# A graph transformer on one NeuronCore: the edges' places come as one row and are spread over the partitions by PE

## The chip, the cores and the metric

One core of a Trainium2 chip. The metric is the device time of one execution, in microseconds, the median of three runs. The profile is of one more execution. Engines: PE (TensorE), DVE (VectorE), ACT (ScalarE), POOL (GpSimd), SP (SyncE, which here only issues DMAs).

## The reference

Two layers of a heterogeneous graph transformer over 6250 nodes (128 features, 8 heads of 16) and 100,000 edges sorted by target, then a projection, a residual and a layer norm. What matters here is the part over edges:

```python
kw = kT[src, :, etype]
m = vT[src, :, etype]
a = jnp.einsum('ehd,ehd->eh', kw, q[dst]) * pri[:, etype].T / SQRT_D
att = edge_softmax(a, dst, n)          # exp(a - max over the edges of dst) / sum of these
msg = (m * att[:, :, None]).reshape(-1, H * HS)
hag = jax.ops.segment_sum(msg, dst, num_segments=n)
```

## The kernel before

Each layer has a matrix stage (`fused`: the tables of keys and values by node and relation, and q, by tiles of 128 nodes) and an edge stage (`attend`). The change touches the edge stage alone.

Edges stand in slots of 128, each slot with edges to the nodes of one tile of 128. Four slots are a quad, eight quads a block, and each layer has 26 blocks, so 208 quads (`NQUADS`), 416 in both layers. The five engines run their own instruction streams through the quads in order and meet on semaphores. For a quad q of a block:

- POOL (L793) gathers four times 128 rows of 1 KB from the table into `rows`, which holds three blocks (`DEPTH`), 24 quads. Before it refills a quad's place it waits for `sum_psum` of 24 quads before (L791).
- SP (`load_places`, L609) loads for each quad the place of each edge in its node tile, 512 bf16 numbers, the same for all 128 partitions, by one DMA of 128 KB with a broadcast source, into a ring of four (`DST_RING`). Per block it also loads two arrays of flags (L602).
- DVE compares these numbers with the partition's number (`turned`, L1750) and so makes `onehotT`, 128 x 512 f32, in a ring of two. It does it for quad q+2 in its step for q.
- PE multiplies that with the tile's q rows (`fetch_q`, L1268), which gives the q of each edge in bank 1 or 2, and tells `q_psum`. In its step for q it does the fetch of q+1.
- DVE multiplies the gathered keys with them (`multiply`, L1742), sums by head (L1755), and some quads later weighs the values (`weigh`, L1764).
- ACT makes the one-hot matrices by edge (L1012, L1015), PE sums the weighed rows into node rows (`sum_quad`, L1281, two pairs of slots a quad, each telling `sum_psum`) 13 quads after their product, DVE adds them to `sums` (L1779).
- In quads 0 to 5 of each block, the maxima over the edges of each node for the block before: DVE's scans, and five small groups of matmuls on PE, some into bank 3 and some into bank 4 (L1295, L1311, L1319, L1325, L1332).

DVE's step for a quad has four places in this order: the product; at place 0 an add, then `turned` for q+2; at place 1 an add and the head sums; at place 2 an add; at place 3 an add and the weighing. A piece of the maxima comes at some of these places.

## Time and profile before

| | us |
|---|---|
| median of three runs (lowest, highest) | 4215.57 (4210.69, 4224.35) |
| the profiled execution | 4224.53, its span 4222.7 |
| busy in the span: PE | 2457.1 (58%) |
| DVE | 2713.9 (64%) |
| ACT | 1710.2 (40%) |
| POOL | 2537.3 (60%) |

Busy shares are means over matrix stages and edge stages, which have different limits, so each is to be read by stretch. "x1664" is a count; behind the first bar of a grouped row stand the busy time in us and the mean ns of one, behind the second the idle time of the engine just before these instructions and what ended it. "remote" stands where the semaphore that ended the wait was updated at a time at which no instruction of the trace ends; "issue" where nothing is seen that was waited for. A `x8` in a timeline row merges eight instructions: an f32 matmul counts twice, so four matmuls are eight.

### The profile page before, as it was taken

Reading aid. Unit: us, or ns where it says so; the run is one execution under the profiler, and the core shown is the slowest. Engines: PE = TensorE matmul, PEld = TensorE weight load, DVE = VectorE, ACT = ScalarE, POOL = GpSimd, SP = SyncE. Lnnn points to the kernel's source line nnn. Section 1 sums busy time; section 2 is a strip of 40 time slices with the busy share of each in tenths; the row PEclk is TensorE's granted clock in tenths of the full one; section 3 lists DMA queues with packets and bytes.
Section 4 is the critical chain, followed back from the end, with each engine's and each line's share of the span. In section 5 each row is a group of like instructions: output and inputs, shape, how many; then the busy total and the mean of one; then the engine's idle time right before and its main releaser. Section 6 shows DMA issues by size and latency. Waiting matters only on the chain.

```text
span 4222.7 us, 54460 instructions
## 1 busy us (share of the span) xinstructions
PE 2457.1 (58%) x12785; PEld 1801.8 (43%) x12786; DVE 2713.9 (64%) x6706; ACT 1710.2 (40%) x3970; POOL 2537.3 (60%) x2596
## 2 busy tenths in 40 slices
PE   3777771455565555656677776145655555555365
PEld 2333331345454545545333333144554545444343
DVE  6676671466676666667678887156666666666465
ACT  2676670233323333324566666023323333323255
POOL 4666657466666666661566664746666666666426
PEclk8899895677777777777789899567777777777666
DMA  8999984344444444434799998434434344444131
GB/s 197 409 414 410 417 338 146 89 119 119 117 128 117 119 117 116 118 113 107 241 383 380 406 398 327 129 88 115 119 111 113 112 114 114 116 113 113 53 111 48
DMA packets 321826, 782.64 MB, mean 185 GB/s; under 512 B 87083, under 2 KB 249803, under 8 KB 309007
## 3 DMA queue, kind: packets, MB, share of 16 engines
q0 software_dynamic: 110672, 651.37, 43.1%
q1 hardware_dynamic: 202387, 127.10, 11.3%
q8 instruction: 126, 2.06, 0.2%
q10 hardware_dynamic: 8448, 0.53, 0.1%
q14 instruction: 193, 1.58, 0.1%
HBM read 335.58 MB, written 573.46 MB: 215 GB/s over the span
## 4 chain that ended last, share of the span: by engine, by line
DVE 19%; PE 18%; issue 18%; another core or an unknown queue 17%; DMA 16%; ACT 4%; DVEq 4%; POOL 3%; SPq 0%; POOLq 0%; ACTq 0%
DMA relation_table<-region,scatter_node 14%; PE bank L1281 7%; DVE sums L1779 6%; PE bank L1268 4%; PE bank L1114 3%; ACT region L876 2%; DVE region L1764 1%; DVEq L1768 1%; DVE region L1742 1%; DVEq L1779 1%; DVE region_q L1750 1%; PE bank L1144 1%; DVE region L1568 1%; PE bank L1319 1%
## 5 line engine op out<-in xcount | busy, mean ns | idle before, releaser
L793 POOL DMA_INDIRECT region<-relation_table,key_of x1664 | 1630.6, 980 | 926.8 <-issue 465.4
L1281 PE MATMUL bank<-region,arena 128*128 128x136 f32 x3328 | 708.9, 377 | 548.7 <-DVE region L1764 270.2
L1281 PEld LDWEIGHTS bank<-region,arena 128*128 128x128 f32 x3328 | 613.3, 267 | 631.1 <-DVE sums L1779 311.5
L1012 ACT ACTIVATE arena<-iota_free,minus_dst 128x128 f32<-128x128 f32 x1664 | 528.5, 388 | 821.9 <-remote 406.9
L1742 DVE TENSOR_TENSOR region<-bank,region 128x512 f32<-128x512 f32 x416 | 285.1, 685 | 895.8 <-remote 659.0
L1114 PE MATMUL bank<-sums,arena 128*128 128x512 bf16 x2048 | 633.6, 420 | 248.0 <-ACT region L876 202.6
L876 ACT COPY region<-bank 128x512 f32<-128x512 f32 x1152 | 624.8, 600 | 357.9 <-DMA relation_table<-region,scatter_node 222.6
L1268 PE MATMUL bank<-region_q 128*128 x3328 | 620.6, 349 | 240.1 <-DVE region L1742 117.3
L1568 DVE COPY region<-bank 128x512 f32<-128x512 f32 x896 | 586.1, 686 | 259.9 <-DMA relation_table<-region,scatter_node 171.9
L1268 PEld LDWEIGHTS bank<-region_q 128*128 128x128 f32 x3328 | 585.9, 263 | 252.8 <-issue 252.1
L1779 DVE TENSOR_TENSOR sums<-sums,bank 128x136 f32 x1664 | 472.9, 284 | 77.0 <-DVE sums L1779 31.3
L1023 ACT ACTIVATE region<-arena 128x256 f32<-128x256 f32 x52 | 21.7, 417 | 1077.0 <-DVE arena L1848 789.8
L1114 PEld LDWEIGHTS bank<-sums,arena 128*128 128x128 bf16 x2048 | 196.6, 103 | 579.9 <-ACT region L876 280.5
L1764 DVE TENSOR_TENSOR region<-region 128x512 f32<-128x512 f32 x416 | 283.9, 683 | 2.2 <-issue 0.2
L1755 DVE TENSOR_REDUCE arena<-region 128x32 f32<-128x512 f32 x416 | 280.4, 674 | 0.1
L1015 ACT ACTIVATE arena<-arena 128x512 f32<-128x512 f32 x416 | 262.0, 630 | 13.1
L717 POOL TENSOR_TENSOR sums<-arena,sums 128x256 f32<-128x256 f32 x128 | 86.2, 673 | 259.3 <-ACT arena L894 256.3
L1750 DVE TENSOR_SCALAR region_q<-arena,row_no 128x512 f32<-128x512 bf16 x416 | 204.7, 492 | 13.8 <-issue 7.0
L1575 DVE COPY arena<-bank 128x1024 bf16<-128x1024 bf16 x256 | 175.5, 686 | 48.0 <-PE bank L1114 13.6
L1135 PE MATMUL bank<-identb,sums 128*128 128x128 bf16 x2048 | 180.7, 239 | 2.9 <-POOL sums L721 2.9
L1135 PEld LDWEIGHTS bank<-identb,sums 128*128 128x128 bf16 x2048 | 156.5, 108 | 56.5 <-issue 18.2
L734 POOL DMA_INDIRECT relation_table<-region,scatter_node x128 | 129.1, 1009 | 72.7 <-issue 35.2
(243 smaller groups left out, 2654.5 us busy)
## 6 DMA issues: line engine op xcount, KB each, us to landing
arena<-edge_places SPq DMA_DIRECT2D x416, 128.0 KB
region<-relation_table,key_of POOLq DMA_INDIRECT x1664
arena<-segment_flags SPq DMA_DIRECT2D x104, 128.0 KB
region_q<-q_rows SPq DMA_DIRECT2D x6, 768.0 KB, 6.5
aggregated_rows<-one_less_alpha SPq DMA_DIRECT2D x17, 256.0 KB
region<-aggregated_rows SPq DMA_DIRECT2D x16, 272.0 KB, 2.8
sums<-relation_weight_parts SPq DMA_DIRECT2D x32, 128.0 KB
x_sorted<-arena SPq DMA_DIRECT2D x16, 256.0 KB
```

The costliest lines, as they stand in the source:

```text
L793: pool.indirect_dma_start(out=rows[:, block_.r, q * QUAD + s], out_offset=None, in_=table, in_offset=bass.IndirectOffsetOnAxis(ap=key_of[: ...
L876: nc.scalar.copy(stage[:, r, :, k * HS:(k + 1) * HS], bank[TABLE_BANK + k % TABLE_BANKS][:, :].rearrange("p (t o) -> p t o", t=RT)).then_i ...
L1012: chain.step(nc.scalar.activation(onehots[:, at, s], iota_free[:, :], ACT.Abs, bias=minus_dst[:, bass.ds(block_.b * BLOCK + (q * QUAD + s) ...
L1114: nc.tensor.matmul(bank[TABLE_BANK + k % TABLE_BANKS][:, :], x_spreadT[:, k, :], w_rel[:, k, :], start=True, stop=True).then_inc(table_psu ...
L1135: ins = nc.tensor.transpose(bank[SPREAD_BANK[half]][:, :].bitcast(BF16)[:, k * P:(k + 1) * P], x_spread[:, tile.par, half * H + k].rearran ...
L1268: ins = nc.tensor.matmul(bank[1 + q % 2][:, s * D:(s + 1) * D], onehotT[:, q % 2, s], q_rows[:, bass.ds(tiles[s], 1), :].rearrange("p a n ...
L1281: ins = nc.tensor.matmul(bank[SUM_BANK[q % 2][pair]][:, s * SUMC:(s + 1) * SUMC], onehots[:, at, 2 * pair + s], rows[:, block_.r, slot, RH ...
L1568: v.tensor_copy(stage[:, r, :, k * HS:(k + 1) * HS], bank[TABLE_BANK + k % TABLE_BANKS][:, :].rearrange("p (t o) -> p t o", t=RT)).then_in ...
L1742: v.tensor_tensor(here, bank[1 + q % 2][:, :].rearrange("p (s d) -> p s d", s=QUAD), here, ALU.mult).then_inc(prod_ready, 1)
L1755: v.tensor_reduce(score[:, block_.par, q * QUAD:(q + 1) * QUAD, :], rows[:, block_.r, q * QUAD:(q + 1) * QUAD, 0:D].rearrange("p s (h o) - ...
L1764: v.tensor_tensor(msg, msg, bc(part[:, :, RHS0:D], 3, HS), ALU.mult).then_inc(weighted, 1)
L1779: v.tensor_tensor(total, total, bank[SUM_BANK[q % 2][n // 2]][:, (n % 2) * SUMC:(n % 2 + 1) * SUMC], ALU.add).then_inc(sum_added, 1)
```

## The change

The places are loaded as one row in one partition, four quads (4 KB) at a time, two DMAs a block. PE spreads a quad's row over all partitions by a matmul with a row of ones, bf16, into bank 4 (`spread_places`, in its step for q for quad q+3), and DVE's `turned` compares out of bank 4. A new semaphore `places_psum` goes from PE to DVE, `ones_ready` from DVE to PE once a layer. All matmuls of the maxima now write to bank 3. The row buffer lies behind `onehotT`, the ring in `arena` is gone.

```diff
-ONEHOT_RING, DST_RING = 3, 4
+ONEHOT_RING, HALF_QUADS = 3, QPB // 2
...
-        places_words = arena[:, o:o + DST_RING * QUAD * P // 2]
-        edge_places = places_words.bitcast(BF16).rearrange("p (r e) -> p r e", r=DST_RING)
-        flags, o = take(arena, o + DST_RING * QUAD * P // 2, 4 * CLEN, "p (r k e) -> p r k e", r=2, k=2)
+        places_words = wqf[:, NTILES * D + 2 * QUAD * P:NTILES * D + 2 * QUAD * P + BLOCK * P // 2]
+        place_row_in = places_words[0:1, :].bitcast(BF16).rearrange("o (q e) -> o q e", q=QPB)
+        flags, o = take(arena, o, 4 * CLEN, "p (r k e) -> p r k e", r=2, k=2)
+        ones_words, o = take(arena, o, P // 2, "p n -> p n")
+        ones_b = ones_words[0:1, :].bitcast(BF16)
...
-                def load_places(i, par, q):
-
-                    quad = (2 * i + par) * QPB + (l * NQUADS + q)
-                    wait(sp, onehotT_ready, quad - (DST_RING - 1))
-                    source = place_rows[bass.ds((2 * i + par) * BLOCK + q * QUAD, QUAD), :].rearrange("s e -> (s e)")
-                    sp.dma_start(edge_places[:, q % DST_RING], bc(source, 0, P)).then_inc(places_in[q % DST_RING], 16)
+                def load_places(b, half):
+
+                    first = half * HALF_QUADS
+                    wait(sp, onehotT_ready, b * QPB + (l * NQUADS + first - HALF_QUADS))
+                    source = place_rows[bass.ds(b * BLOCK + first * QUAD, HALF_QUADS * QUAD), :].rearrange("s e -> (s e)")
+                    into = place_row_in[:, first:first + HALF_QUADS].rearrange("o q e -> o (q e)")
+                    sp.dma_start(into, source.unsqueeze(0)).then_inc(places_in[half], 16)
...
-                        for q in range(QPB):
-                            load_places(i, par, q)
+                        for half in range(2):
+                            load_places(b, half)
...
+                def spread_places(block_, q):
+
+                    quad = block_.quad(l, q)
+                    pe.wait_ge(places_in[q // HALF_QUADS], 16 * block_.b + 16 * (l * NBLOCKS + 1))
+                    wait(pe, onehotT_ready, quad)
+                    nc.tensor.matmul(bank[4][:, :], ones_b[:, :], place_row_in[:, q], start=True, stop=True).then_inc(places_psum, 1)
...
-                        nc.tensor.matmul(bank[4][:, 0:H], cross_hot[:, :], lower[:, :], start=True, stop=True).then_inc(rescale_psum, 1)
+                        nc.tensor.matmul(bank[3][:, 0:H], cross_hot[:, :], lower[:, :], start=True, stop=True).then_inc(rescale_psum, 1)
...
+                        later_ = ahead(block_, q, 3)
+                        if later_[0].real:
+                            spread_places(*later_)
...
+                pe.wait_ge(ones_ready, l + 1)
+                for q in range(2):
+                    spread_places(Block(0, 0), q)
                 fetch_q(Block(0, 0), 0, slot_tiles(0, 0))
+                spread_places(Block(0, 0), 2)
...
-                    dve.wait_ge(places_in[q % DST_RING], 16 * (block_.b * (QPB // DST_RING)) + 16 * (l * NBLOCKS * (QPB // DST_RING) + q // DST_RING + 1))
+                    dve.wait_ge(places_psum, quad + 1)
                     wait(dve, q_psum, quad - 1)
                     flat = onehotT[:, q % 2].rearrange("p s e -> p (s e)")
-                    v.tensor_scalar(flat, edge_places[:, q % DST_RING], row_no[:, 0:1], None, ALU.is_equal).then_inc(onehotT_ready, 1)
+                    v.tensor_scalar(flat, bank[4][:, :], row_no[:, 0:1], None, ALU.is_equal).then_inc(onehotT_ready, 1)
...
+                v.memset(ones_b, 1.0).then_inc(ones_ready, 1)
```

## Rows read from the trace of the kernel before

**Rows 1.** Window: busy us of PE, PEld, DVE, ACT, POOL, then clock, DMA share.
```profile
1100.00:1800.00 700.00, 409.50 (x2114) 360.85 (x2114) 461.01 (x1264) 221.09 (x598) 452.72 (x460) 0.73 0.42 118
```

**Rows 2.** Waits of POOL (total us, times, longest), 1100 to 1800 us; then whole span.
```profile
POOL region L793 <- issue: 126.3, 404, 1.5
POOL region L793 <- remote: 76.9, 31, 3.1
POOL region L793 <- PE bank L1281: 44.1, 25, 2.9
...
POOL region L793 <- remote: 241.9, 95, 3.3
POOL region L793 <- PE bank L1281: 208.3, 90, 35.6
```

**Rows 3.** The page's costliest groups: product, compare, a copy from a bank.
```profile
L1742 DVE TENSOR_TENSOR region<-bank,region 128x512 f32<-128x512 f32 x416 | 285.1, 685 | 895.8 <-remote 659.0
...
L1568 DVE COPY region<-bank 128x512 f32<-128x512 f32 x896 | 586.1, 686 | 259.9 <-DMA relation_table<-region,scatter_node 171.9
...
L1750 DVE TENSOR_SCALAR region_q<-arena,row_no 128x512 f32<-128x512 bf16 x416 | 204.7, 492 | 13.8 <-issue 7.0
```

**Rows 4.** Gathers until 760 us, products until 770 us: count, min/median/max ns, starts.
```profile
L793 POOL DMA_INDIRECT region<-relation_table,key_of x95: 945/949/1119, 641.2 to 759.3; - x95
...
L1742 DVE TENSOR_TENSOR region<-bank,region x8: 692/693/693, 649.2 to 763.9; 128x512 f32<-128x512 f32 x8
```

**Rows 5.** Timeline of 670 to 766 us: start, us, instruction, idle before and its releaser.
```profile
675.05 0.69 DVE L1742 TENSOR_TENSOR region<-bank,region 128x512 f32<-128x512 f32 x1 [13.78 <-remote]
...
676.16 89.21 SPq L609 DMA_DIRECT2D arena<-edge_places  x5
...
676.28 2.07 PE L1268 MATMUL bank<-region_q 128*128 x8 [13.39 <-DVE region L1742]
...
697.97 2.07 PE L1268 MATMUL bank<-region_q 128*128 x8 [19.62 <-DVE region L1742]
...
719.14 0.69 DVE L1742 TENSOR_TENSOR region<-bank,region 128x512 f32<-128x512 f32 x1 [20.72 <-remote]
...
720.50 2.07 PE L1268 MATMUL bank<-region_q 128*128 x8 [20.46 <-DVE region L1742]
...
741.54 0.69 DVE L1742 TENSOR_TENSOR region<-bank,region 128x512 f32<-128x512 f32 x1 [20.59 <-remote]
...
763.94 0.69 DVE L1742 TENSOR_TENSOR region<-bank,region 128x512 f32<-128x512 f32 x1 [20.72 <-remote]
```

**Rows 6.** Timeline of 1384 to 1400 us.
```profile
1385.62 1.91 PE L1268 MATMUL bank<-region_q 128*128 x8
...
1388.45 2.18 PE L1281 MATMUL bank<-region,arena 128*128 128x136 f32 x8 [0.91 <-issue]
...
1390.42 1.92 PE L1268 MATMUL bank<-region_q 128*128 x8
...
1393.45 0.95 POOL L793 DMA_INDIRECT region<-relation_table,key_of  x1 [0.30 <-issue]
1396.57 0.69 DVE L1742 TENSOR_TENSOR region<-bank,region 128x512 f32<-128x512 f32 x1 [9.91 <-remote]
1396.78 1.28 ACT L1012 ACTIVATE arena<-iota_free,minus_dst 128x128 f32<-128x128 f32 x4 [8.88 <-remote]
...
1397.43 0.95 POOL L793 DMA_INDIRECT region<-relation_table,key_of  x1 [3.04 <-remote]
```

**Rows 7.** Waits of DVE in the first matrix stage, 100 to 640 us.
```profile
DVE region L1568 <- PE bank L1114: 53.9, 103, 2.3
```

**Rows 8.** PE's matmuls of 512 bf16 columns: count, min/median/max ns.
```profile
L1114 PE MATMUL bank<-sums,arena x2048: 376/379/634, 77.2 to 2628.5; 128*128 128x512 bf16 x187
```

**Rows 9.** What ended DVE's idle time before the compare, L1750: us, times.
```profile
  DMA arena<-edge_places: 6.7, 2
```

**Rows 10.** DMA queues of the page: packets, MB, share of 16 engines.
```profile
q0 software_dynamic: 110672, 651.37, 43.1%
q1 hardware_dynamic: 202387, 127.10, 11.3%
```

More of the change, by code:

```diff
@@ L273, in gnn_kernel @@
         places_stored = sem("places_stored")
-        places_in = [sem(f"places_in{i}") for i in range(DST_RING)]
+        places_in = [sem(f"places_in{i}") for i in range(2)]
+        places_psum, ones_ready = sem("places_psum"), sem("ones_ready")
         q_psum, prod_ready, score_ready = sem("q_psum"), sem("prod_ready"), sem("score_ready")
@@ L1318, in step @@
                         for n, column in enumerate((fwd[:, CLEN - 1:CLEN], first_seg[:, CLEN - 1:CLEN], bwd[:, 0:1], last_seg[:, 0:1])):
-                            ins = nc.tensor.matmul(bank[4][0:1, n * P:(n + 1) * P].rearrange("o (h j) -> o h j", h=H),
+                            ins = nc.tensor.matmul(bank[3][0:1, n * P:(n + 1) * P].rearrange("o (h j) -> o h j", h=H),
                                                    column, by_head, start=True, stop=True)
@@ L1324, in step @@
                         for n in range(2):
-                            ins = nc.tensor.matmul(bank[4][:, n:n + 1], carry_rows[0:1, n].rearrange("o j h -> o (j h)"),
+                            ins = nc.tensor.matmul(bank[3][:, n:n + 1], carry_rows[0:1, n].rearrange("o j h -> o (j h)"),
                                                    ones[0:1, 0:1], start=True, stop=True)
@@ L1784, in scale_crossing @@
                     dve.wait_ge(rescale_psum, b + (l * NBLOCKS + 1))
-                    link(v.tensor_scalar(rescale[:, :], bank[4][:, 0:H], 1.0, None, ALU.add))
+                    link(v.tensor_scalar(rescale[:, :], bank[3][:, 0:H], 1.0, None, ALU.add))
                     wait(dve, sum_added, b * BLOCK + l * NQUADS * QUAD)
@@ L1816, in find_maxima @@
                         dve.wait_ge(chunk_rows, before + 1)
-                        got = bank[4][0:1, :].rearrange("o (k h j) -> o k h j", k=4, h=H)
+                        got = bank[3][0:1, :].rearrange("o (k h j) -> o k h j", k=4, h=H)
                         for n in range(2):
@@ L1835, in find_maxima @@
                         dve.wait_ge(carry_T, before + 1)
-                        chain.step(v.tensor_copy(chunk_carry[:, :], bank[4][:, 0:2]))
+                        chain.step(v.tensor_copy(chunk_carry[:, :], bank[3][:, 0:2]))
                     if (q, place) == (3, 1):
```

## The prediction

> **What bounds the kernel now.** I read the windows first, then the waits of GpSimd and VectorE, then two stretches of the timeline. The change touches only the two edge stages (`attend`, one for each layer), which begin near 641 and 2637 us; the stages between them keep their instructions.
>
> In 700 us of the first edge stage [rows 1] GpSimd issues 460 gathers, 4 for a quad, so 115 quads, one in 6.09 us. A gather takes 0.984 us (452.72 / 460), and 126.3 / 460 = 0.275 us of issue [rows 2] lie before the next, so four need 5.04 us. VectorE is busy 461.0 us, 4.0 us a quad, PE 409.5 us, 3.6 us a quad. No engine is full. GpSimd is nearest to it; what it lacks are waits for the sums whose row buffers it refills [rows 2]: 76.9 + 44.1 = 121.0 us in the stretch, 1.05 us a quad, and 241.9 + 208.3 = 450 us in both stages. 5.04 + 1.05 is the period. VectorE stands idle 896 us in all before its product with q L1742 [rows 3].
>
> What does L1742 wait for? For the gathered rows and for `q_psum`, PE's fetch of q. At the start of the stage GpSimd has issued 95 gathers, over 23 quads, by 759 us, while VectorE has done 8 products by 764 us [rows 4]: the rows are there. PE's fetches take 2.07 us [rows 5], and each is issued right behind the product two before the one that needs it. Yet the product at 719.14 us, whose fetch ran from 676.28 to 678.35 us, comes 40.8 us after its end, that at 741.54 us 41.5 us after, that at 763.94 us 41.4 us after: two fetches are always under way, and one result is seen in 22.4 us. In the middle of the stage [rows 6] PE is through with a fetch (1387.5), two pairs of sums (1390.6) and another fetch (1392.3); VectorE, ScalarE and GpSimd, each waiting for one of these, all begin at 1396.6 to 1397.4, over 2 us after GpSimd's last gather (1393.45 to 1394.40) had used up the free buffers. The releaser is called "remote" since no row of PE ends near. In the matrix stages PE hands 128x512 results over without this: 103 waits of the copies last 53.9 us together, the longest 2.3 us [rows 7]. **So the bound is a loop:** while GpSimd gathers without a pause PE's results are seen late; the sums are then late too, GpSimd runs out of freed buffers, and in its pause the results come through, several at once.
>
> **The change, part by part**, for 416 quads. The sum is made against the profiled execution, 4224.5 us (its span is 4222.7), 8.9 above the median of 4215.6.
>
> The **compare** (L1750) will read 128x512 f32 out of PSUM and not bf16 out of SBUF. It takes 492 ns now [rows 3]. The nearest rows are the copy of 128x512 f32 out of a bank and the product with one operand in a bank, 686 and 685 ns [rows 3]; a compare with a scalar out of a bank is the like of the copy, so 0.69 us, and 0.20 x 416 = +82 us of VectorE work. VectorE is idle a third of the stage, which covers most; it costs where VectorE catches up after a release. Bounds 0 and +82, I take a third: +27.
>
> **PE** gets one bf16 matmul of 512 columns a quad. The nearest row has 128x512 bf16 at 379 ns in the median [rows 8]: 416 x 0.38 = 158 us of PE work. It stands behind the fetch and ahead of the next sums, and PE is idle 2.5 us a quad, in waits for VectorE. Bounds 0 and +158; I take 0.
>
> **The waits on PE.** The spread of quad q+3 waits for the landed half row and for the compare of q+2, which VectorE does at place 0 of the same step. Queued behind it on PE are that step's small matmuls for the maxima and the next quad's sums, for which GpSimd and VectorE's adds wait. Each of them needs something that VectorE does later in the step (a scan, a carry, the weighing at place 3), so this wait never ends last: 0.
>
> **The wait on VectorE** is the dear part. The compare now waits for `places_psum`, one more result that PE has to hand over in each quad. Queued behind it on VectorE are the head sums, the adds, the weighing, and through them PE's sums and GpSimd's buffers. Before, the compare needed a fetch already used by the product just ahead of it; a VectorE held up stopped only at a product. Now it can stop at the compare too. PE hands over 1 fetch, 2 pairs of sums and 5 results a block of 8 quads for the maxima, 3.6 a quad; this becomes 4.6, +28%. Bounds: nothing, as the spread's result follows right behind that of the fetch for which the product ahead waits anyway; and the whole share of the idle time before L1742, 896 x 0.28 = +251 us. I take the share of what GpSimd waits, as its pace is the period: 450 x 0.28 = +126.
>
> **DMA and SyncE.** 416 loads of 128 KB become 104 of 4 KB into one partition. The compares wait 6.7 us for loads now, in 2 waits [rows 9]. The new loads are issued 4 quads, 24 us, ahead and are as hidden. SyncE's issues stand on nobody's path: 0. What less traffic might give is in rival D.
>
> **GpSimd's gathers** have a median of 949 ns and a mean of 984 [rows 1, 4]. Had the compare caused all that lies above the median, it would be 35 ns x 1664 = 58 us; weighing, product, adds and scans run beside gathers too, so I take a third, -20, bounds 0 and -58. The Trainium skill (SBUF — State Buffer, section "Who interferes with whom") speaks for the change here: a scalar compare from SBUF to SBUF can run in a two-port mode that locks GpSimd out of the port it shares with VectorE, and one that reads PSUM can't. By that rule the compare's share ends with the change.
>
> The maxima's move to bank 3 adds no instruction and no wait, the memset of ones comes once a layer: 0.
>
> **Sum:** 27 + 0 + 126 - 20 = +133, so 4216 + 133, about **4350 us**.
>
> **Rivals.** (B) *Each added result costs its full share.* At a stage's start one result came through in 22.4 us [rows 5]; with two a quad VectorE does half as many quads before GpSimd stops, and later its idle time grows with their number: 251 + 27 - 20 = +258, or 4474, with a part of PE's 158 us near 4500. For it: the one-by-one rows. Against: several results come at once in [rows 6].
> (C) *Covered.* The spread's result comes with the fetch's and the compare's 0.2 us is eaten by idle time: 4216 + 27 - 20 = 4223, within 0.3%. For it: VectorE's idle third.
> (D) *Faster, the other side.* GpSimd sets the pace and loses its disturbances: -58 if the compare was their cause; and if the 128 KB loads were part of what makes PE's results late, a share of GpSimd's 450 us goes too. Their queue has 11.3 of the 54.4% that queues 0 and 1 hold of the DMA engines [rows 10]: 450 x 11.3 / 54.4 = -93. 4216 - 58 - 93 + 27 = 4092, half of that gain 4150. It decides if the results come earlier by more than the added one holds them up, 28% of the wait. Against: SyncE issues one such load in each of the 22.4 us steps [rows 5], and there the delay is longest.
> (E) *It doesn't do what it says:* the 4 KB into one partition land so late that PE waits at each half block. It would have to take over 24 us; folded into A.
>
> **Chances.** A, my forecast, 0.55 (on its own 4270 to 4430); B 0.14; C 0.12; D 0.19. The range takes in A, C, most of B and the near part of D: 4180 to 4500. A measurement of this kernel tells about 0.3% (13 us) from no change. Slower by more: A and B, 0.69. Within: C, 0.12. Faster: D, 0.19.
>
> **What the profile after would show.** The compare at 0.69 us. GpSimd's waits for sums near 576 us (A), 450 (C) or under 360 (D). A new group of idle time before the compare, and with what stays before L1742 more than 896 us (A, B). Products in the first 100 us of a stage 45 us apart under B, 22.4 under C. Gathers nearer to 0.949 us in the mean. The forecast is wrong if the idle time before the compare is small and that before L1742 is what it was, for then PE's results come in groups and one more costs nothing; or if both shrink, for then the loads had a part in the delay.

## The result and the profile after

The changed kernel takes 4244.45 us (median of 8 runs, 4235.31 to 4249.63), the kernel before on the same chip 4224.66 us (8 runs): a ratio of 1.0049, 95% interval 1.0037 to 1.0062, so **slower by 20 us, 0.5%**. The forecast was 4350. Two later comparisons of the same pair gave 1.0075 (1.0061 to 1.0089) and 1.0042 (1.0026 to 1.0059): 16 to 32 us. The direction held; the size was wrong by a factor of four to eight. The time lies in the whole range, 4180 to 4500, and below that of A alone, 4270 to 4430.

The window of the first edge stage and GpSimd's waits, as in [rows 1, 2] (the sums' line is now L1292, the gathers' L797); of the waits those of the whole span:

```profile
1100.00:1800.00 700.00, 440.97 (x2196) 351.20 (x2195) 481.77 (x1249) 222.32 (x601) 448.12 (x457) 0.74 0.34 96
```

```profile
POOL region L797 <- issue: 465.8, 1474, 1.4
...
POOL region L797 <- remote: 260.4, 100, 3.3
POOL region L797 <- PE bank L1292: 207.5, 88, 39.5
```

457 gathers instead of 460 in the window. GpSimd waits 467.9 us for sums instead of 450.2 [rows 2], +18; my forecast had 576. The groups that answer to [rows 3], with the gathers and the added matmul (busy us, mean ns, then idle time before it and what ended it):

```profile
L1760 DVE TENSOR_TENSOR region<-bank,region 128x512 f32<-128x512 f32 x416 | 284.4, 684 | 811.8 <-remote 618.5 <-PE bank L1279 109.4 <-issue 82.3
...
L1768 DVE TENSOR_SCALAR region_q<-bank,row_no 128x512 f32<-128x512 f32 x416 | 309.5, 744 | 67.5 <-remote 36.6 <-issue 30.9
...
L1271 PE MATMUL bank<-region_q,arena 1*128 1x512 bf16 x416 | 199.8, 480 | 676.4 <-DVE region_q L1768 534.7 <-issue 127.5 <-DMA region_q<-edge_places 14.1
...
L797 POOL DMA_INDIRECT region<-relation_table,key_of x1664 | 1624.4, 976 | 945.1 <-issue 465.8 <-remote 260.4 <-PE bank L1292 207.5
```

The compare takes 744 ns, 252 more than before. The idle time before it grew from 13.8 [rows 3] to 67.5 us, while that before the product fell from 895.8 [rows 3] to 811.8 us: together VectorE is idle there for 879 us, less than before. PE now idles before the spread (534.7 us for the compare). Its idle time before the sums fell, of which the wait for the weighing was 270.2 us before and is 126.7 now; the page before and after:

```profile
L1281 PE MATMUL bank<-region,arena 128*128 128x136 f32 x3328 | 708.9, 377 | 548.7 <-DVE region L1764 270.2
...
L1292 PE MATMUL bank<-region,arena 128*128 128x136 f32 x3328 | 683.1, 366 | 277.6 <-DVE region L1782 126.7
```

The queue of the loads fell from 11.3% [rows 10] to:

```profile
q1 hardware_dynamic: 142691, 72.98, 6.6%
```

Where the 25.1 us between the two spans lie, by the starts of GpSimd's gathers in each stage (count, min/median/max ns, first and last start):

```profile
L797 POOL DMA_INDIRECT region<-relation_table,key_of x832: 940/946/1449, 644.3 to 1923.1; - x167
...
L797 POOL DMA_INDIRECT region<-relation_table,key_of x832: 940/946/1457, 2650.8 to 3928.2; - x167
```

Before, they ran from 641.2 to 1913.1 and from 2637.0 to 3909.3. So 1278.8 and 1277.4 us against 1271.9 and 1272.3: +12.0 for both. Of that +6.2 lies in the first 96 gathers of the stages and the wait behind them (159.3 and 157.9 us against 155.2 and 155.8), and only +5.8 in the other 736 of both stages together. The rest is +3.1 ahead of the first gather, +3.8 between the stages, and +6.2 behind the last gather. A second profile of the changed kernel (v1, below) repeats the first two parts, +5.8 and +5.6, but not the rest: +0.4, -3.1 and +4.9. So the whole change, with the longer compare in it, costs 0.016 us a quad in the steady part, where I had spread 0.30 us over each of the 416 quads for the handshake alone.

The start of the stage tells most. The timeline of VectorE, the products and the compares (start, us, instruction, idle before it and its releaser), which answers to [rows 5]:

```profile
679.29 0.69 DVE L1760 TENSOR_TENSOR region<-bank,region 128x512 f32<-128x512 f32 x1 [16.23 <-remote]
683.42 0.75 DVE L1768 TENSOR_SCALAR region_q<-bank,row_no 128x512 f32<-128x512 f32 x1 [3.44 <-issue]
...
704.49 0.69 DVE L1760 TENSOR_TENSOR region<-bank,region 128x512 f32<-128x512 f32 x1 [19.73 <-issue]
708.62 0.75 DVE L1768 TENSOR_SCALAR region_q<-bank,row_no 128x512 f32<-128x512 f32 x1 [3.44 <-remote]
...
729.69 0.69 DVE L1760 TENSOR_TENSOR region<-bank,region 128x512 f32<-128x512 f32 x1 [19.73 <-issue]
```

The products lie 25.2 us apart, not 22.4 [rows 5] and not the 45 of rival B. The compare waits 3.4 us behind each product: it starts 4.1 us after the product that the fetch's result released. And in the steady part, in the pause of GpSimd that ends at 1390.03:

```profile
1389.44 0.69 DVE L1760 TENSOR_TENSOR region<-bank,region 128x512 f32<-128x512 f32 x1 [3.07 <-remote]
1390.03 0.94 POOL L797 DMA_INDIRECT region<-relation_table,key_of  x1 [2.35 <-PE bank L1292]
...
1391.23 0.75 DVE L1768 TENSOR_SCALAR region_q<-bank,row_no 128x512 f32<-128x512 f32 x1
```

The compare follows with no idle time before it: the results came through together, the spread's with them.

### The profile page after: what moved, and what is told of

Read it like the earlier page. It is cut to its first block, busy times and chain, and to the rows that moved or that the text cites. A ratio compares the mean times of both kernels' runs of the same rounds, so it can differ in the third digit from the quotient of the medians.

```text
span 4247.8 us, 55334 instructions
## 1 busy us (share of the span) xinstructions
PE 2616.7 (62%) x13201; PEld 1807.7 (43%) x13202; DVE 2814.7 (66%) x6708; ACT 1710.2 (40%) x3970; POOL 2529.6 (60%) x2596
## 4 chain that ended last, share of the span: by engine, by line
DVE 21%; issue 20%; PE 16%; another core or an unknown queue 15%; DMA 15%; ACT 5%; DVEq 4%; POOL 3%; SPq 0%; ACTq 0%; POOLq 0%
DMA relation_table<-region,scatter_node 14%; DVE sums L1797 6%; PE bank L1292 5%; PE bank L1279 3%; PE bank L1118 3%; ACT region L880 2%; DVE region L1782 2%; DVE region L1760 2%; DVEq L1786 2%; DVE region_q L1768 1%; DVEq L1797 1%; ACT arena L1016 1%; PE bank L1148 1%; DVE region L1586 1%
## 5 line engine op out<-in xcount | busy, mean ns | idle before, releaser
L797 POOL DMA_INDIRECT region<-relation_table,key_of x1664 | 1624.4, 976 | 945.1 <-issue 465.8
L1292 PE MATMUL bank<-region,arena 128*128 128x136 f32 x3328 | 683.1, 366 | 277.6 <-DVE region L1782 126.7
L1760 DVE TENSOR_TENSOR region<-bank,region 128x512 f32<-128x512 f32 x416 | 284.4, 684 | 811.8 <-remote 618.5
L1292 PEld LDWEIGHTS bank<-region,arena 128*128 128x128 f32 x3328 | 582.1, 255 | 388.0 <-issue 186.7
L1271 PE MATMUL bank<-region_q,arena 1*128 1x512 bf16 x416 | 199.8, 480 | 676.4 <-DVE region_q L1768 534.7
L1271 PEld LDWEIGHTS bank<-region_q,arena 1*128 1x128 bf16 x416 | 39.3, 94 | 755.5 <-issue 455.8
L1768 DVE TENSOR_SCALAR region_q<-bank,row_no 128x512 f32<-128x512 f32 x416 | 309.5, 744 | 67.5 <-remote 36.6
```

Of the source, the lines that this page charges most:

```text
L797: pool.indirect_dma_start(out=rows[:, block_.r, q * QUAD + s], out_offset=None, in_=table, in_offset=bass.IndirectOffsetOnAxis(ap=key_of[: ...
L1292: ins = nc.tensor.matmul(bank[SUM_BANK[q % 2][pair]][:, s * SUMC:(s + 1) * SUMC], onehots[:, at, 2 * pair + s], rows[:, block_.r, slot, RH ...
L1760: v.tensor_tensor(here, bank[1 + q % 2][:, :].rearrange("p (s d) -> p s d", s=QUAD), here, ALU.mult).then_inc(prod_ready, 1)
L1768: v.tensor_scalar(flat, bank[4][:, :], row_no[:, 0:1], None, ALU.is_equal).then_inc(onehotT_ready, 1)
```

## The experiments

Ratios are to the kernel before, run beside each kernel on the same chip, since it takes 4223 to 4254 us from one comparison to another (3719 in that of y4). 0.1% is 4.2 us. Traces of runs from different comparisons differ by this too. The kernels x1 to x4, x8, w2, y3, y4 and t2 leave out the loads or the gathers and serve for timing alone.

| kernel | median us | ratio (95%) |
|---|---|---|
| x1_no_loads | 4246.99 | 0.9998 (0.9988 to 1.0008) |
| x2_psum_compare | 4268.79 | 1.0052 (1.0035 to 1.0069) |
| x3_pe_only | 4246.61 | 0.9996 (0.9987 to 1.0006) |
| x4_pe_handshake | 4254.75 | 1.0017 (1.0007 to 1.0026) |
| w2_pe_handshake (x4 again) | 4252.81 | 1.0008 (0.9999 to 1.0018) |
| x6_four_tiny | 4242.90 | 1.0041 (1.0025 to 1.0056) |
| x7_bf16_fetch | 4156.53 | 0.9837 (0.9822 to 0.9852) |
| w3_bf16_fetch (x7 again) | 4180.11 | 0.9834 (0.9819 to 0.9849) |
| z1_bf16_pairs | 4231.92 | 1.0016 (1.0007 to 1.0025) |
| x8_no_gathers | 3329.73 | one run |
| y1_one_add | 4270.98 | 1.0037 (1.0026 to 1.0049) |
| y2_wide_add | 4270.92 | 1.0045 (1.0029 to 1.0060) |
| y3_wait_at_once | 4415.35 | 1.0390 (1.0361 to 1.0418) |
| y4_wait_late, where the kernel before takes 3719 | 3732.12 | 1.0040 (1.0028 to 1.0053) |
| w1_the_change | 4280.90 | 1.0075 (1.0061 to 1.0089) |
| v1_the_change | 4239.03 | 1.0042 (1.0026 to 1.0059) |
| t1_change_bf16 | 4225.15 | 0.9928 (0.9912 to 0.9945) |
| t2_compare_bf16 | 4195.84 | 0.9874 (0.9857 to 0.9890) |

### One part of the change at a time

**x1_no_loads**: the kernel before, the wide loads issued for the first four quads of a layer only, and the compare reading these over again. The added lines:

```diff
+                    if 2 * i + par or q >= DST_RING:
+                        return
```

> The kernel before without the 128 KB loads of places: only the first four quads of a layer are loaded, every later compare reads what lies in the ring (the output is then not the reference's). Nothing waits for a load any more. Theory R (in the pauseless gathering at a stage's start PE finishes one pair of weight load and matmul in 2.8 us, whatever else runs): the loads have no part in that, the first products stay 22.4 us apart and the time falls by 0 to 20 us. Rival L (the loads make PE's results late, and their removal hid the cost of the new compare and spread): products nearer than 20 us apart and a fall of 60 us or more.

4 us or less either way: the loads' removal is worth nothing in time. Rival D's second half is out: with their queue at 6.6%, the first products still lie 22.4 us apart.

```profile
713.93 0.69 DVE L1744 TENSOR_TENSOR region<-bank,region 128x512 f32<-128x512 f32 x1 [20.71 <-remote]
736.34 0.69 DVE L1744 TENSOR_TENSOR region<-bank,region 128x512 f32<-128x512 f32 x1 [20.73 <-remote]
```

**x2_psum_compare**: x1, with the compare out of a bank that VectorE fills once a layer, and no added matmul.

```diff
-                    v.tensor_scalar(flat, edge_places[:, q % DST_RING], row_no[:, 0:1], None, ALU.is_equal).then_inc(onehotT_ready, 1)
+                    v.tensor_scalar(flat, bank[4][:, :], row_no[:, 0:1], None, ALU.is_equal).then_inc(onehotT_ready, 1)
```

> As x1_no_loads, and the compare reads bank 4, which is filled once a layer; the maxima are all in bank 3; no matmul is added. It measures the compare out of PSUM alone: 744 ns and not 492, +105 us of VectorE work. Covered by idle time (theory R): 0 to +20 us over x1_no_loads. If a third of it counts, as I had predicted: +35 us. First products 22.4 us apart.

```profile
L1753 DVE TENSOR_SCALAR region_q<-bank,row_no 128x512 f32<-128x512 f32 x416 | 308.5, 742 | 0.1
```

104 us of added VectorE work (308.5 less 204.2 in x1) cost 0.54%, 23 us. That is the size of the whole change's cost. What the compare reads changed in two ways at once, from SBUF to a bank and from bf16 to f32; no run tells which of the two made it longer.

**x3_pe_only**: x1 with the spread matmul, which nobody waits for. **x4_pe_handshake**: also the waits of both sides, the compare still out of SBUF.

```diff
+                    wait(pe, onehotT_ready, quad)
+                    nc.tensor.matmul(bank[4][:, :], ones_b[:, :], edge_places[0:1, 0], start=True, stop=True).then_inc(places_psum, 1)
...
+                    dve.wait_ge(places_psum, quad + 1)
```

> As x1_no_loads, with one matmul of 512 bf16 columns a quad on PE into bank 4 in the place of the spread; nobody reads its result or waits for it, and it waits for nothing; the maxima are in bank 3. Theory R: the first products are 25.2 us apart (9 pairs in place of 8, at 2.8 us) though VectorE waits for no added result, and the time rises by 5 to 20 us over x1_no_loads. Rival W (the step is the count of results or waits and the 25.2 us of the changed kernel came with its wait): 22.4 us apart and the time of x1_no_loads.

> As x3_pe_only, but the matmul waits for the compare before it and the next compare waits for the matmul, as in the changed kernel; the compare still reads SBUF. Theory R: as x3_pe_only within 10 us, since the result comes with the fetch's. The forecast's reason (one more handed-over result costs 126 us): +100 us or more over x3_pe_only.

The matmul is free in time (0.9996 against 0.9998), though it moves the first products from 22.4 to 25.2 us apart (x3):

```profile
724.20 0.69 DVE L1760 TENSOR_TENSOR region<-bank,region 128x512 f32<-128x512 f32 x1 [23.52 <-remote]
749.45 0.69 DVE L1760 TENSOR_TENSOR region<-bank,region 128x512 f32<-128x512 f32 x1 [23.58 <-remote]
```

The handshake costs 0.19% against x1, 8 us, and 0.08% in the repeat, 3 us, where the interval takes in no cost at all:

> The kernel with one spread matmul a quad and the waits both ways, the compare from SBUF, the loads left out but for the first four, as before. Delaying chip: +8 us (0.2%). Chip without the delay: 0 to +13 us, as in the kernel that waited at the end of the step (+13 us there), GpSimd without waits.

This is the term that I had put at +126.

### What one more result costs

A pass here is one load of weights with its matmul. An f32 matmul takes two, so a fetch of four f32 matmuls is eight passes and the spread, in bf16, is one.

**x6_four_tiny**: the kernel before with four more matmuls of 8 columns behind each fetch.

```diff
+                    for s in range(4):
+                        nc.tensor.matmul(bank[4][:, 8 * s:8 * s + 8], identb[:, :], identb[:, 0:8], start=True, stop=True)
```

> The kernel before, with four more matmuls of 8 bf16 columns behind each fetch of a quad, into a bank that nobody reads in the edge stages. Count theory (while GpSimd issues gathers without a pause, TensorE completes one pair of weight load and matmul pass in 2.8 us, whatever its size): the first products of an edge stage lie 22.4 + 4 x 2.8 = 33.6 us apart instead of 22.4, the start of a stage is longer by up to 10 us, and behind it, where GpSimd pauses, nothing is seen; 4225 to 4250 us. Rival, delay by work: four matmuls of 8 columns are 0.1 to 0.2 us of TensorE, so the first products stay 22.4 us apart and the time is the before's. Second rival, the share I forecast by (GpSimd's 450 us of waits grow with the number of TensorE's results that come late): 12 passes where 8 were, half as many again, so +100 us or more.

```profile
687.48 0.69 DVE L1744 TENSOR_TENSOR region<-bank,region 128x512 f32<-128x512 f32 x1 [26.60 <-remote]
721.08 0.69 DVE L1744 TENSOR_TENSOR region<-bank,region 128x512 f32<-128x512 f32 x1 [31.92 <-remote]
754.68 0.69 DVE L1744 TENSOR_TENSOR region<-bank,region 128x512 f32<-128x512 f32 x1 [31.92 <-remote]
```

33.6 us apart, to the digit: 22.4 plus 4 x 2.8. Four matmuls of next to no work delay as four large ones would, so it is their number that counts. In time they cost 17 us, not 100.

**x7_bf16_fetch**: the fetch in bf16, with `onehotT` in bf16 and the upper half of each word of q (q is cut to bf16 there), so 4 passes of PE a quad and not 8. **z1_bf16_pairs**: the same `onehotT`, and q split by one VectorE subtraction a part into an upper and a lower bf16 half, 8 bf16 passes. x7's line:

```diff
-                                               q_rows[:, bass.ds(tiles[s], 1), :].rearrange("p a n -> p (a n)"), start=True, stop=True)
+                                               q_pairs[:, bass.ds(tiles[s], 1), :, 1].rearrange("p a n -> p (a n)"), start=True, stop=True)
```

> The kernel before with the fetch of q in bf16: the one-hot matrix is bf16 and only the upper half of each q word is multiplied, so a fetch is 4 pairs of weight load and matmul instead of 8, and q is cut to bf16 (this part of the computation is changed). Count theory: the first products lie 4 x 2.8 = 11.2 us apart instead of 22.4, and a stage's start is shorter by some 8 us of waits at most. The compare writes bf16 instead of f32: if the written width sets it, it falls below its 0.49 us, to 0.3 us or so, which by the fifth of the compare's change that counted in the comparison of before and after is 416 x 0.19 x 0.2 = 16 us less. Together 4195 to 4215 us. Rival, TensorE's latency binds the steady part of the edge stage too: half of the fetch's passes gone takes 100 us or more off GpSimd's waits, 4120 us or less. Second rival: the products' distance is set by the columns of the fetch: also about half, so x6 tells these two apart and not this one.

> The kernel before with q split in place into an upper and a lower bf16 half by one VectorE subtraction for each loaded part, and each fetch as two accumulating bf16 matmuls instead of one f32 matmul; the one-hot matrix is bf16. Eight pairs of weight load and matmul as before, so by the count theory the first products stay 22.4 us apart. The compare writes bf16, as in the kernel with the bf16 fetch: 10 to 20 us less if its duration falls to 0.3 us; four subtractions a stage cost a few us on VectorE between the stages. 4205 to 4225 us. Rival, the written width does not matter: compare stays at 0.49 us and the time is the before's or 5 us more.

```profile
681.69 0.69 DVE L1743 TENSOR_TENSOR region<-bank,region 128x512 f32<-128x512 f32 x1 [4.76 <-remote]
692.20 0.69 DVE L1743 TENSOR_TENSOR region<-bank,region 128x512 f32<-128x512 f32 x1 [8.96 <-remote]
703.40 0.69 DVE L1743 TENSOR_TENSOR region<-bank,region 128x512 f32<-128x512 f32 x1 [9.65 <-remote]
```

From 681.69 on 10.5 and 11.2 us apart, as 4 x 2.8 says; the first six products were nearer, 4.3 to 5.6 us, in step with their gathers. So the delay isn't there from the first gather on: before, the products start at 649.25, 653.67, 659.55, 675.05 and 696.74 us, and lie 22.4 us apart only from there. A little later in x7 the small f32 matmuls of the maxima join in:

```profile
722.05 2.01 PE L1320 MATMUL bank<-ident,arena 128*1 128x128 f32 x8 [16.20 <-issue]
724.00 0.61 PE L1269 MATMUL bank<-region_q 128*128 x4
...
731.39 0.69 DVE L1743 TENSOR_TENSOR region<-bank,region 128x512 f32<-128x512 f32 x1 [9.39 <-issue]
...
764.99 0.69 DVE L1743 TENSOR_TENSOR region<-bank,region 128x512 f32<-128x512 f32 x1 [9.42 <-remote]
```

Their 8 passes and the fetch's 4 put two products 33.6 us apart, 12 x 2.8, the distance that x6 has. The time was a miss: I expected 4195 to 4215, it is 4156.5, with GpSimd's waits at 241.8 + 157.8 = 399.6 us instead of 450.2. z1 tells that this isn't the width: its compare falls as far (148.9 us busy, 358 ns), its matmuls are bf16 too and its fetches keep PE busy for 405.9 us instead of 620.6, but there are 8 passes, and it gains nothing (+7 us; the eight subtractions are 15.1 us of VectorE ahead of the stages). So passes taken away gain more (four of them 68 us) than passes added cost (four of them 17, one none).

**x8_no_gathers**: the kernel before without the gathers of the edge stages, all other work kept.

```diff
-                        pool.indirect_dma_start(out=rows[:, block_.r, q * QUAD + s], out_offset=None, in_=table,
```

> The kernel before without the gathers of the edge stages (the row buffers keep what they hold), so that GpSimd issues nothing there; all other engines do all of their work. Theory that TensorE's results are late only while GpSimd issues gathers: the products come as soon as VectorE is ready, none of the 22.4 us distances is left, and the stage runs at VectorE's pace: busy 461 of 700 us in the window, so about 0.7 x 1356 = 950 us a stage instead of 1356, and the whole at 3400 us or so. Rival, TensorE's own pace of 2.8 us a pass (its sequencer, or its weight loads): the first products stay 22.4 us apart, and the stage gains little.

```profile
650.08 0.69 DVE L1738 TENSOR_TENSOR region<-bank,region 128x512 f32<-128x512 f32 x1 [1.85 <-PE bank L1265]
...
651.78 0.69 DVE L1738 TENSOR_TENSOR region<-bank,region 128x512 f32<-128x512 f32 x1
...
653.48 0.69 DVE L1738 TENSOR_TENSOR region<-bank,region 128x512 f32<-128x512 f32 x1
...
655.08 0.68 DVE L1738 TENSOR_TENSOR region<-bank,region 128x512 f32<-128x512 f32 x1
```

1.6 to 1.7 us apart, VectorE without a pause; the time is 3330, where I had expected 3400 or so. Of these two the delay is there only in the kernel that gathers. The run takes away GpSimd's issuing and the gathers' transfers together, so it doesn't tell which of them delays PE's results.

### VectorE's longer work

**y1_one_add** and **y2_wide_add**: the kernel before with one more VectorE operation a quad behind the compare, an add from SBUF into unused room, 128x128 or 128x512. y2's lines:

```diff
+                    wait(dve, added, quad)
+                    fourfold = bc(ident[:, :], 1, 4)
+                    v.tensor_tensor(spare.rearrange("p (k n) -> p k n", k=4), fourfold, fourfold, ALU.add).then_inc(added, 1)
```

> The kernel before with one more VectorE operation a quad right behind the compare: an add of 128x128 f32 from SBUF into unused room, about 0.2 us, that nobody waits for. Theory of VectorE's time (the compare costs what its longer work costs, whether it reads PSUM or not): in the kernel that compares out of PSUM 104 us of added VectorE work cost 22 us, a fifth; so 416 x 0.2 = 83 us of work cost some 17 us: 4240 us against 4223. Rival, it is the read of PSUM (a bank that TensorE and VectorE both use) and not the time: the before's time within 5 us.

> The same with the add on 128x512 f32 (about 0.69 us, 285 us of added VectorE work). Theory of VectorE's time with a fixed share of a fifth: +60 us. If the share grows once VectorE's idle time is eaten: +100 to +200 us. Rival, PSUM alone: less than +20 us.

118.1 us of work (284 ns each) cost 0.37%, 284.0 us (683 ns each) 0.45%, with intervals that overlap. The first is 17 us, as I expected, but I had expected it for 83 us of work; by the share of x2 118 us would have cost 0.6%. So VectorE's time can explain most of the compare's 0.54% (0.35 to 0.69, against 0.26 to 0.49 for y1), and the intervals leave open whether all of it; a small effect of the bank is not ruled out. The second is a miss: the cost isn't proportional. y2's waits and gathers:

```profile
POOL region L795 <- remote: 233.7, 94, 3.4
POOL region L795 <- PE bank L1283: 176.2, 68, 37.9
```

```profile
L795 POOL DMA_INDIRECT region<-relation_table,key_of x1664 | 1696.3, 1019 | 897.5 <-issue 475.9 <-remote 233.7 <-PE bank L1283 176.2
```

The gathers grow to 1019 ns, +66 us in all against the trace of before, and GpSimd's waits fall by 40 to 410 us. In y1, from the same comparison as y2, the gathers take 983 ns and the waits are 476.2 us. Most of what GpSimd loses in a gather it no longer has to wait.

### Where the result is waited for

**y3_wait_at_once**: x4, but VectorE waits for the spread in the step of the compare that PE waits for, right behind the head sums, not a step later. **y4_wait_late**: the same at the end of that step.

```diff
-                    dve.wait_ge(places_psum, quad + 1)
...
                             head_sums(block_, q)
+                            coming = ahead(block_, q, 3)
+                            if coming[0].real:
+                                dve.wait_ge(places_psum, coming[0].quad(l, coming[1]) + 1)
```

> The kernel with the handshake both ways (loads left out but for the first four, one spread matmul a quad into a bank, the compare from SBUF), but VectorE waits for the spread's result in the same step, right behind the head sums, some 1 us after the compare that TensorE waits for before it issues the spread; before it waited one step (6 us) later. Theory that the handshake was nearly free (+8 us) because the result has a whole step to come and comes with the fetch's: now it can't, each quad has a second round trip to TensorE, and in the stretches in which GpSimd gathers without a pause each costs some us: +60 to +200 us. Rival, a result of TensorE costs little wherever it is waited for: within 15 us of the kernel before. My forecast's price for one more result handed over was +126 us, with no regard to the distance.

```profile
POOL region L798 <- issue: 542.8, 1461, 4.0
POOL region L798 <- PE bank L1292: 488.4, 196, 42.7
...
POOL region L798 <- remote: 12.7, 5, 2.8
```

3.9%, +166 us (the medians differ by 161), for the same result as in x4 with +8 or +3. GpSimd's waits are 501 us, and the time put down to its issue rises from 472.6 (x4) to 542.8. The granted clock of PE is lower too, 0.63 between 1100 and 1800 us against 0.75 in x4, and a pass of the fetch takes 400 ns instead of 343; how much of the 166 us comes by that, the run doesn't tell. So a price of my forecast's order does exist, for a result that VectorE asks for and waits for at once.

> As the kernel in which VectorE waits for the spread's result right behind the head sums (+166 us against the kernel before), but the wait stands at the end of the same step, just ahead of the next quad's product, for whose fetch VectorE waits anyway; the spread is the next thing on TensorE behind that fetch. (Loads left out but for the first four; compare from SBUF.) Theory that the price of a result is set by what VectorE has to do meanwhile and by which result it waits for anyway: near the +8 us of the wait that stands behind that product, 8 to 40 us. Rival, each wait inside the step of the request costs a round trip: +100 us or more.

+13 us, in the range that I gave. But in this comparison the kernel before takes 3718.83 us (11 runs, 3709 to 3724), and in y4's trace the delay doesn't exist:

```profile
POOL region L798 <- issue: 504.8, 1656, 0.3
...
DVE region L1761 <- DMA region<-relation_table,key_of: 404.7, 353, 3.9
```

```profile
661.37 0.69 DVE L1761 TENSOR_TENSOR region<-bank,region 128x512 f32<-128x512 f32 x1 [2.93 <-DMA region<-relation_table,key_of]
666.48 0.69 DVE L1761 TENSOR_TENSOR region<-bank,region 128x512 f32<-128x512 f32 x1 [3.43 <-issue]
671.57 0.69 DVE L1761 TENSOR_TENSOR region<-bank,region 128x512 f32<-128x512 f32 x1 [3.40 <-issue]
```

GpSimd waits for nobody, the products come 5.1 us apart, in step with four gathers, and the gathers alone are the bound. This run therefore says nothing on y3's question, and how y4 does where the delay is stays open. I called this "a chip without the delay"; that it is the chip is not shown. y4 ran on a chip numbered 6, and so did x1 to x4 and w1 to w3, with the delay and with 4247 and 4249 us for the kernel before; whether that is the same chip is not known.

Two more comparisons of the change itself, expected for either case, met the delay:

> The changed kernel once more, beside the kernel before on the same chip. On a chip that delays TensorE's results (before at 4220 to 4260 us, first products 22.4 us apart): +0.5% again, products 25.2 us apart. On a chip that does not (before near 3720 us): GpSimd's gathers follow one another without a wait and alone set the pace, so neither the longer compare nor the handshake can cost; what is left is the 5 us between the stages and the gathers' mean: from -10 us (gathers 4 to 6 ns shorter, 1664 of them, the wide loads gone) to +10 us. Rival: the change costs its 20 us there as well, and the delay had nothing to do with them.

> The changed kernel beside the kernel before. Delaying chip (before at 4220 to 4260 us): +0.4 to +0.8%, products 25.2 us apart. Chip without the delay (before near 3720 us): GpSimd's gathers alone set the pace, so -10 to +10 us; rival, the change costs its 20 to 30 us there too.

0.75% and 0.42%, products 25.2 us apart in both. On one chip and in one comparison the whole change (w1, 1.0075) stands 0.67%, 28 us, above the handshake with the compare out of SBUF (w2, 1.0008). Why the change stands at 16, 20 and 32 us in three comparisons stays open, and what it costs where there is no delay was not seen.

### The change on top of the bf16 fetch

**w3_bf16_fetch** is x7 again, **t1_change_bf16** the changed kernel with x7's fetch, **t2_compare_bf16** is x2 with it (compare out of PSUM, no spread).

> The kernel with the fetch in bf16 of the upper half of each word of q (q cut to bf16 in the fetch), 4 passes of TensorE a quad instead of 8. Delaying chip: -1.6% again. Chip without the delay: GpSimd's gathers set the pace, so nothing: within 8 us of the before. If it gains 60 us there too, TensorE's passes cost by another way than the delay.

> The changed kernel with the fetch of the bf16 kernel (one-hot matrix in bf16, upper half of each word of q, q cut to bf16). Delaying chip: the bf16 fetch alone stands at -1.6%, the change alone at +0.4 to +0.75%; if they add, -1.0% (4180 to 4210 us where the before is 4225 to 4250). If the spread's pass costs by the count of passes (a fifth more instead of a ninth), or if the compare's duration no longer falls with a narrower result, less: -0.6% or so. Chip without the delay (before near 3720 us): GpSimd's gathers set the pace and both changes are worth nothing, -15 to +10 us; rival there, the change costs its 20 us.

> The kernel with the bf16 fetch (q cut to bf16) and the compare out of a bank that VectorE fills once a layer; no spread matmul, no added wait, loads left out but for the first four. Delaying chip: if the compare carries the cost here too, -0.7 to -0.8%, as with the whole change on top of the bf16 fetch (-0.72%); if the spread's pass and wait do, -1.5% or so, as the bf16 fetch alone. Chip without the delay (before near 3720 us): the compare out of PSUM is then beside GpSimd's gathers alone and costs nothing, -15 to +5 us; rival, its 20 us are there as well.

```profile
709.26 0.69 DVE L1761 TENSOR_TENSOR region<-bank,region 128x512 f32<-128x512 f32 x1 [9.25 <-remote]
...
723.26 0.69 DVE L1761 TENSOR_TENSOR region<-bank,region 128x512 f32<-128x512 f32 x1 [9.23 <-remote]
...
737.27 0.69 DVE L1761 TENSOR_TENSOR region<-bank,region 128x512 f32<-128x512 f32 x1 [9.24 <-remote]
```

14.0 us apart: five passes of 2.8. Here the change costs 0.9% (0.9928 against 0.9834 and 0.9837), about 39 us: the compare 0.4% of it (0.9874), the spread and its handshake the other 0.5%, 23 us. These ratios come from four comparisons. For t1 the second of my cases came out (-0.6% expected, -0.72% measured), for which I had named two reasons, the count of passes and a compare that no longer gets shorter; the compare did stay at 743 ns, and by t2 both have a part. For t2 neither of my two cases did, it lies between them. Where the fetch has four passes, one more with its wait costs more than where it has eight.

**x7 is the fastest of the kernels run** that do all of the work, 1.6% under the kernel before and 2.1% under the changed one, at the price of q cut to bf16 in the fetch.

## Why the prediction was wrong in size

**The bound** was read rightly: PE's results are late while GpSimd gathers, and come through in its pauses. x8 shows it. What I missed is the unit. Where the delay has set in at a stage's start, each pass takes a slot of 2.8 us, whatever its size: distances of 11.2, 14.0, 22.4, 25.2 and 33.6 us for 4, 5, 8, 9 and 12 passes. The fetch's 2.07 us row with its x8 [rows 5] had the 8 in it; 22.4 / 8 was there to be worked out, and with it the 25.2.

**The handshake, +126**, is the step that failed: 28% more results, taken as 28% more of GpSimd's 450 us of waits. It measured +8 and +3 (x4, w2). Two things were wrong in it. I counted results handed over, and not passes: the spread is 1 pass beside 8 of the fetch and 8 of the sums. A share by passes would have been too dear as well: x6 adds 4 to these 16, a quarter of 450 us by that reckoning, and costs 17. And I gave every result the same price wherever it is waited for. The spread stands right behind a fetch for which VectorE waits anyway, and VectorE needs it a step later: the compare stood 3.4 us in the first stretch and not at all in the pause shown. I had written that as the lower bound ("the spread's result follows right behind that of the fetch") and didn't take it, though [rows 6] showed several results at once. y3 is the case in which such a share would have been near the truth (+166). The idle time before the compare is small, 67.5 us, and the sum of both is 879 us and not more than 896: both were my own signs that the forecast is wrong. But that before the product shrank, and for this I had written that the loads had a part in the delay; x1, without the loads, has 916.0 us of it, so that reading of the sign was wrong.

**The compare, +27**: measured +23 (x2 against x1) on a duration that I had too short, 744 ns and not 686. The copy out of a bank was the wrong neighbour by 58 ns. So 104 us of work, of which a fifth counts, not 82 of which a third does. The two errors nearly cancel, which is luck, and y1 and y2 show that a fixed share is no law: 118 us cost 17 and 284 us cost 19.

**PE's matmul, 0**: right (x3, 0.02% apart), at 480 ns a piece instead of 380. **PE's waits, 0**: right in effect, by what x4 and w2 cost with both waits. They moved from the sums (270.2 us for the weighing, then 126.7) to the spread (534.7).

**The loads, 0**: right (x1). **The gathers, -20**: 980 to 976 ns, -6 us (v1's profile has 970). Of that x1 without the loads has 1628.4 us and x2 with the compare out of the bank 1623.3, so the compare's part is 5 us of the 58 that I had as the bound. The rule that I cited from the Trainium skill (SBUF — State Buffer, "Who interferes with whom") says that a scalar compare outside the two-port modes doesn't hold GpSimd up; the trace agrees in sign at most, since its 3 ns a gather are less than three profiles of the changed kernel differ by (976, 977 and 970).

**The rivals.** C had the mechanism (covered, results come with the fetch's) and came nearest, with 4223; its +7 falls short by the -20 for the gathers, not by its +27 for the compare, which the measured +23 is near and which has the compare's part of the gathers in it. The parts as measured, +23 for the compare and +3 to +8 for the handshake, make +26 to +31, against +16, +20 and +32 for the whole: the intervals of the single parts, about 0.1% or more each way, allow no closer sum. B and D are out: products 25.2 us apart, not 45; loads worth nothing.

What isn't settled: by what way gathers delay PE's results, and why only after the first few products of a stage; why the cost of the same change differs between 0.42% and 0.75%, why 0.28 us of VectorE a quad costs as much as 0.68; and why four passes fewer gain four times what four more cost.

## What to carry to other kernels

Where results come late on a queue, ask what stands just ahead of the new one and whether it is waited for anyway, and how far behind its request it is needed; the same matmul and semaphore cost 3 to 8 us or, waited for at once, 166. A count of results times a share of some idle time isn't a price. When a long wait recurs with one length, divide it by the number of instructions in the group: 22.4 / 8 gave the law of the first stretch, and pointed to the edit that gained 1.6% (fewer passes of PE). An operand moved from SBUF to a bank, in f32 instead of bf16, can cost VectorE more than the transfer it saves: 492 became 744 ns, and the 128 KB loads that it replaced had cost nothing.

## What the runs showed of the hardware

- At the start of an edge stage, while GpSimd issues indirect gathers back to back, what PE hands over comes in one pass of 2.8 us after another, 8 columns or 512. It sets in some 20 to 50 us after the first gather (first products 4 to 6 us apart). Without gathers the same products come every 1.6 us (x8).
- In one comparison this delay was absent: 3719 us for the kernel before, 12% less than elsewhere, and in y4's trace 1.8 us of GpSimd's waits for sums. The gathers are no shorter there (997 ns in the mean of y4, against 982 in x4). Whether this belongs to the chip, and what differs, these traces don't tell.
- A VectorE add of 128x512 f32 from SBUF lengthened GpSimd's gathers by 39 ns in the mean (y2); an add of 128x128 left them at 983 (y1). y2's whole loss was 19 us, since GpSimd's waits shrank. The same page and section of the Trainium skill hold that an add with two inputs from SBUF takes only a read port that descriptor generation doesn't need, which they call inferred; by that inference the gathers would have kept their 980 ns, and they didn't. The same section also holds that a VectorE instruction with two inputs from SBUF contends with a GpSimd instruction that reads SBUF; a gather reads its keys there, so this may be the way. No run parts the two.
- A bf16 result shortened the compare out of SBUF from 492 to 358 ns; out of a bank it takes 743 or 744 ns, to bf16 (t1) or f32 (the change).
